# Convolutions on zero-padded or stacked rows in place of 32-row matmuls, and image 1 prepared later

## The reference, cut to what matters

```python
x = x + L0(gn(x), ...)      # gn: mean and variance over the 48x48 of each channel
x = x + dct2(gn(x))         # 48x48 cosine transforms along both axes

# in L0, per image
embed_w  = prelu(Wa @ x + ba)              # 32 -> 32 channels, full size; 6x6 patches, stride 2
match_in = prelu(W1 @ x + b1)              # 32 -> 16 channels, full size; 3x3 patches (queries)
ref      = prelu(W2 @ mean2x2(x) + b2)     # 32 -> 16 channels, 24x24; 3x3 patches (576 keys)
norm     = maximum(sqrt(sum(w * w)), 1e-4) # one per key
yi       = softmax(10 * (w / norm) @ queries, over the 576 keys)   # 576 x 2304
yt       = transposed convolution of yi with the patches of embed_w
yd       = (conv3x3(yt, Wd, stride 2) + bd) / 6
```

## Time and profile before

| | |
|---|---|
| median of 3 runs | 312.26 us (311.34 to 315.21) |
| the profiled execution | 313.37 us, of which its span is 311.6 us |
| mean granted TensorE clock | 0.863 of full |
| busy share of the span | PE 82%, PEld 76%, DVE 51%, ACT 42%, POOL 31% |
| instructions | 4697, 1698 of them matmuls |

### The profile page before, as it was taken

How to read it: one execution, slowest core, us unless ns; L and a number is a source line. 1 busy time by engine, 2 the same in 40 slices (tenths; PEclk the granted TensorE clock), 3 DMA queues, 4 the chain that set the end, 5 groups by cost and what they waited for, 6 DMA issues and landing times.

```text
span 311.6 us, 4697 instructions
## 1 busy us (share of the span) xinstructions
PE 255.3 (82%) x1698; PEld 237.3 (76%) x1698; DVE 160.0 (51%) x343; ACT 130.9 (42%) x257; POOL 96.8 (31%) x98
## 2 busy tenths in 40 slices
PE   0458749966599999959989999999989899997085
PEld 0336748955588889949989899999978799996073
DVE  7544163247544363662266446467787664434722
ACT  2053035376346662442256846365646422121020
POOL 6220150077265343144041344339619200000000
PEclk9999999576555895985799999999999999999555
DMA  3430444000003004440000000000300000000321
GB/s 91 108 52 1 70 72 68 1 1 0 3 0 52 2 0 69 68 70 6 2 0 3 0 2 0 2 1 0 78 1 2 0 2 2 0 2 1 63 50 38
DMA packets 11494, 7.67 MB, mean 25 GB/s; under 512 B 8496, under 2 KB 10608, under 8 KB 11344
## 3 DMA queue, kind: packets, MB, share of 16 engines
q1 hardware_dynamic: 11168, 6.94, 12.3%
q10 hardware_dynamic: 304, 0.45, 0.4%
HBM read 2.14 MB, written 1.18 MB: 11 GB/s over the span
## 4 chain that ended last, share of the span: by engine, by line
PE 62%; DVE 21%; issue 8%; ACT 7%; POOL 1%; DVEq 0%; ACTq 0%; POOLq 0%
PE zt L730 21%; PE ps L710 8%; PE yt L745 8%; PE pm L662 6%; PE pm L622 4%; DVE negm L1174 3%; PE pm L684 3%; PE pm L777 3%; DVE yl L1189 3%; PE pd L757 2%; DVE bnst L993 2%; ACT nt L899 2%; DVE v L1212 2%; PE zt L710 2%; PE pm L693 2%
## 5 line engine op out<-in xcount | busy, mean ns | idle before, releaser
L730 PE MATMUL zt<-ident,nt 128*125 128x128 f32 (+1 forms) x720 | 94.8, 284 | 0.0
L730 PEld LDWEIGHTS zt<-ident,nt 128*125 128x125 f32 (+1 forms) x720 | 90.8, 186 | 1.1 <-issue 0.2
L526 POOL TENSOR_TENSOR nt<-nt 128x599 f32<-128x599 f32 (+1 forms) x42 | 56.2, 1338 | 46.9 <-ACT nt L907 39.7
L1189 DVE TENSOR_TENSOR yl<-zt,yh 125x384 fp32r<-125x384 f32 (+1 forms) x60 | 33.4, 556 | 46.6 <-ACT yh L915 15.3
L915 ACT ACTIVATE yh<-zt 125x384 fp32r<-125x384 f32 (+1 forms) x60 | 29.2, 487 | 46.9 <-PE zt L730 46.8
L899 ACT ACTIVATE nt<-ps,negm 128x576 f32<-128x576 f32 x32 | 23.8, 745 | 47.5 <-DVE negm L1174 47.5
L907 ACT ACTIVATE nt<-nt,rps 128x599 f32<-128x599 f32 x36 | 28.7, 798 | 11.8 <-DVE rps L1181 11.5
L516 POOL TENSOR_TENSOR ml<-vim,mh 128x384 fp32r<-128x384 f32 x12 | 12.3, 1029 | 65.3 <-ACT mh L871 65.2
L745 PE MATMUL yt<-yh,kh 125*128 125x384 f32 (+1 forms) x60 | 24.7, 411 | 7.1 <-DVE yl L1189 7.0
L1212 DVE SCALAR_TENSOR_TENSOR v<-pd,v 32x384 f32<-32x384 f32 (+3 forms) x48 | 26.2, 547 | 4.1 <-PE pd L757 2.7
L1174 DVE TENSOR_REDUCE negm<-ps 128x1 f32<-128x576 f32 x32 | 24.1, 753 | 7.6 <-PE ps L710 7.5
(11 more groups left out here) (160 smaller groups left out, 433.1 us busy)
## 6 DMA issues: line engine op xcount, KB each, us to landing
vim<-mimg SPq DMA_DIRECT2D x24, 72.0 KB, 2.5
v<-mimg SPq DMA_DIRECT2D x36, 24.0 KB, 1.9
v<-x SPq DMA_DIRECT2D x2, 288.0 KB, 4.0
vim<-mimg SPq DMA_DIRECT2D x12, 48.0 KB, 2.2
x_copy<-v SPq DMA_DIRECT2D x2, 288.0 KB, 3.1
xr<-x_copy SPq DMA_DIRECT2D x4, 144.0 KB, 2.9
out<-res SPq DMA_DIRECT2D x8, 72.0 KB, 2.2
x<-x SPq DMA_DIRECT2D x6, 72.0 KB, 2.0
```

The source lines that it names most:

```text
L526: pool.tensor_tensor(nt[:, dst, (to + 1) * KP + 1:(to + 1) * KP + 1 + n], nt[:, one, (row1 + 1) * KP + 1:(row1 + 1) * KP + 1 + n], nt[:, o ...
L730: last = nc.tensor.matmul(turned(zt[:, m % 2, :], n, dh, col, JW), keys_at(tile, r + dr, n, shift), ident[:, :], start=at == 0, stop=at == ...
L1189: nc.vector.tensor_tensor(yl[0:n, blk, :].rearrange("p (h j) -> p h j", j=W), turned(zt[:, m % 2, :], n), F(yh[0:n, blk, :]).rearrange("p ...
```

## The change

- **Convolutions of image 0.** conv1 and conv2 contract all 128 rows of x4 (or of its pooled form x2) with weights that are zero outside one quarter (wb1, wb2). They are plain f32 matmuls, one a group or half group, and x is not split for them.
- **Convolutions on stacked parts.** x of an image is loaded three times into 96 rows (x3f). x3 holds its high part in rows 0 to 31 and 64 to 95, and its low part in rows 32 to 63; the weights hold high, high and low. One fp32r matmul of 96 rows gives the sum of the three products. embed of both images and conv1 of image 1 use it; embed has 4 matmuls of 288 columns a group. New jobs are xh (ACT, two halves), xl (DVE, two halves) and wst (DVE).
- **Row sums.** POOL adds the squares of three rows in two additions (sv), and norm has 6 matmuls.
- **Biases.** Three jobs in place of one, placed where each is needed. That of embed is one f32 matmul.
- **Banks.** Ahead of the loop the groups rotate over four banks (pm, yt, pd).
- **Keys.** Scaling, high and low parts go in two halves.
- **Zeroing.** The edges of the tiles (nt), mr and wr are zeroed by ACT; before, POOL and DVE did this.
- **Queues.** x4 is one buffer, so that x of image 1 is loaded after conv1 of image 0. The three copies of image 0 take that place in SP's order, those of image 1 stand behind the patches of image 0. The ninth taps of block 0 are started by ACT. POOL's preparation of the output weights comes after the query splits.
- **Later.** The jobs of image 1 move by up to 5 thirds of a step.

```diff
-    ("xs", (0,)), ("mean", (0,)), ("weights", (0,)), ("bias", (0, 1)), ("conv2", (0, 1)), ("low", (0,)),
+    ("xs", (0,)), ("mean", (0,)), ("weights", (0,)), ("bias_2", (0,)), ("conv2", (0, 1)), ("bias_1", (0,)),
     ("conv1", (0, 1)), ("squares", (0,)), ("conv1", (2, 3, 4, 5, 6, 7)), ("norm", (0,)),
-    ("inorm", (0, 1)), ("keys", (0,)), ("split", (0, 1)), ("bias", (2,))]
+    ("inorm", (0, 1)), ("ninth", (0,)), ("xh", (0, 1)), ("keys", (0, 1)), ("split", (0, 1))]
 
 
 SPREAD = [
-    ("emb", 0, 2, 4, 2), ("ek", 0, 2, 9, 2), ("xs", 1, 1, 13, 1), ("mean", 1, 1, 15, 1), ("weights", 1, 1, 19, 1),
-    ("bias", 1, 3, 22, 1), ("residual", 0, 1, 28, 1), ("conv2", 1, 2, 26, 1), ("low", 1, 1, 27, 1),
-    ("conv1", 1, 8, 29, 1), ("squares", 1, 1, 31, 1), ("norm", 1, 1, 37, 1), ("inorm", 1, 2, 40, 1),
-    ("keys", 1, 1, 42, 1), ("emb", 1, 2, 46, 2), ("ek", 1, 2, 51, 2), ("residual", 1, 1, 60, 1),
+    ("wst", 0, 1, 1, 1), ("xl", 0, 2, 1, 1), ("bias_a", 0, 1, 3, 1), ("emb", 0, 2, 6, 3), ("ek", 0, 2, 12, 2),
+    ("xs", 1, 1, 16, 1), ("mean", 1, 1, 19, 1), ("xh", 1, 2, 20, 1), ("xl", 1, 2, 22, 1), ("weights", 1, 1, 22, 1),
+    ("bias_2", 1, 1, 24, 1), ("wst", 1, 1, 25, 1), ("bias_1", 1, 1, 26, 1), ("conv2", 1, 2, 26, 1), ("bias_a", 1, 1, 28, 1),
+    ("residual", 0, 1, 28, 1), ("conv1", 1, 8, 30, 1), ("squares", 1, 1, 30, 1), ("norm", 1, 1, 35, 1),
+    ("inorm", 1, 2, 39, 1), ("keys", 1, 2, 42, 1), ("emb", 1, 2, 47, 2), ("ek", 1, 2, 52, 2), ("residual", 1, 1, 60, 1),
     ("stats", 0, 6, 91, 1), ("deviation", 0, 1, 98, 1), ("x1n", 0, 3, 102, 2), ("zn", 0, 3, 108, 1),
...
-            x4 = [tmp(f"x4_{b}", [128, QUARTER]) for b in range(B)]
-            x4h = tmp("x4h", [128, QUARTER], F32R)
-            x4l = tmp("x4l", [128, QUARTER], F32R)
+            x4 = [tmp("x4", [128, QUARTER])] * B
+            x3f = tmp("x3f", [96, Q])
+            x3 = tmp("x3", [96, Q], F32R)
...
             return ap.bitcast(F32)
 
+        def bank(n):
+
+            if n < nbefore:
+                return (pm[:, 0, :], pm[:, 1, :], yt[:, :], pd[:, :])[n % 4]
...
+                if b:
+                    sp.wait_ge(s_mf, misc_no["conv1", b - 1, ROWS - 1] + 1)
...
+            def load_copies(b):
+
+                if b:
+                    sp.wait_ge(s_xl[b - 1], 2)
+                for k in range(3):
+                    sp.dma_start(x3f[C * k:C * (k + 1), :],
+                                 x[b].rearrange("c h w -> c (h w)")).then_inc(s_x3[b], 16)
...
             load_x(0, range(2))
             output_weights()
-            load_x(1, range(4))
+            load_copies(0)
             for b in range(B):
                 sp.dma_start(x1(b), x[b].rearrange("c h w -> c (h w)")).then_inc(s_xin[b], 16)
             sp.dma_start(cosm[:, :], dct).then_inc(s_cos, 16)
             ref_patches(0)
+            load_x(1, range(4))
             match_patches(0)
+            load_copies(1)
...
-                pool.memset(nt[:, :, 0:KP], 0.0).then_inc(s_tiles, 1)
-                pool.memset(nt[:, :, PT - KP - 2:], 0.0).then_inc(s_tiles, 1)
-                pool.memset(strided(nt[:, 0, :], KP, (PT, NTILES), (KP, HL)), 0.0).then_inc(s_tiles, 1)
...
                 pool.wait_ge(s_sqp[b], 1)
+                pool.wait_ge(s_sq[b], 2)
+                link(pool.tensor_tensor(sv[:, :], sq[:, 1:1 + L], sq[:, 1 + WL:1 + WL + L], ALU.add))
+                pool.tensor_tensor(sv[:, :], sv[:, :], sq[:, 1 + 2 * WL:1 + 2 * WL + L], ALU.add).then_inc(s_sv[b], 1)
+                pool.wait_ge(s_sv[b], 1)
...
+            def bias_2(b, _):
+
+                pe.wait_ge(s_wb2[b], 1)
+                o = misc("bias_2", b, 0)
+                nc.tensor.matmul(o[0:96, 0:1], wb2[:, 0, :], gm[b][:, 2:3], start=True, stop=True).then_inc(s_mf, 1)
...
                 for k in range(2):
-                    q = 2 * i + k
-                    rows = slice(C * q, C * (q + 1))
-                    if k:
-                        other_rows(last)
-                    last = conv(o[0:96, REFQ * k:REFQ * (k + 1)], q, S_W2, 96, x2h[rows, :], x2l[rows, :])
+                    last = nc.tensor.matmul(o[0:96, REFQ * k:REFQ * (k + 1)], wb2[:, 2 * i + k, :], x2[:, :],
+                                            start=True, stop=True)
                 last.then_inc(s_mf, 1)
 
             def conv1(b, i):
-                if i == 0:
-                    pe.wait_ge(s_wst[b], 1)
-                    pe.wait_ge(s_x4l[b], 1)
+
                 o = misc("conv1", b, i)
-                q, cols = i // 2, slice(HALF * (i % 2), HALF * (i % 2 + 1))
-                rows = slice(C * q, C * (q + 1))
-                conv(o[0:96, 0:HALF], q, S_W1, 96, x4h[rows, cols], x4l[rows, cols]).then_inc(s_mf, 1)
+                if b == 0:
+                    pe.wait_ge(s_wb1, 1)
+                    pe.wait_ge(s_x4[b], 16 * 4)
+                    last = nc.tensor.matmul(o[0:96, 0:HALF], wb1[:, i // 2, :],
+                                            x4[b][:, HALF * (i % 2):HALF * (i % 2 + 1)], start=True, stop=True)
+                else:
+                    pe.wait_ge(s_wst[b], 2)
+                    pe.wait_ge(s_xl[b], i // 4 + 1)
+                    last = nc.tensor.matmul(o[0:96, 0:HALF], wst1[:, :], x3[:, HALF * i:HALF * (i + 1)], start=True,
+                                            stop=True)
+                last.then_inc(s_mf, 1)
 
             def embed(b, i):
 
-                pe.wait_ge(s_wst[b], 2)
+                pe.wait_ge(s_wst[b], 1)
+                pe.wait_ge(s_xl[b], i + 1)
                 o = misc("emb", b, i)
-                for k in range(2):
-                    q = 2 * i + k
-                    rows = slice(C * q, C * (q + 1))
-                    if k:
-                        other_rows(last)
-                    dst = o[:, REFQ * k:REFQ * (k + 1)]
-                    parts = [v[rows, :].rearrange("p (i u j v) -> p i u j v", u=2, j=WL, v=2) for v in (x4h, x4l)]
-                    for n in range(4):
-                        at = S_WA + C * (3 - n)
-                        for m, (w, v) in enumerate(((wsh, 0), (wsh, 1), (wsl, 0))):
-                            last = nc.tensor.matmul(dst, w[rows, at:at + 128], parts[v][:, :, n // 2, :, n % 2],
-                                                    start=n + m == 0, stop=n == 3 and m == 2)
+                v = x3[:, HALFQ * i:HALFQ * (i + 1)].rearrange("p (i u j v) -> p i u j v", u=2, j=WL, v=2)
+                for n in range(4):
+                    at = C * (3 - n)
+                    last = nc.tensor.matmul(o[:, 0:HALF], wsta[:, at:at + 128], v[:, :, n // 2, :, n % 2],
+                                            start=n == 0, stop=n == 3)
...
                 for n in range(6):
-                    for r in range(3):
-                        at = WL * r + 96 * n + 1
-                        last = nc.tensor.matmul(o[0:96, n:n + 1], sq[:, at:at + 96], ones[0:96, 0:1], start=r == 0,
-                                                stop=r == 2)
...
+                zero(nt[:, :, 0:KP], s_tiles)
+                zero(nt[:, :, PT - KP - 2:], s_tiles)
+                zero(strided(nt[:, 0, :], KP, (PT, NTILES), (KP, HL)), s_tiles)
+                zero(mr[:, :, :], s_zero)
+                for b in range(B):
+                    zero(wr[b][:, :], s_zero)
...
+            def x3_high(b, i):
...
                 if b:
                     act.wait_ge(s_mf, misc_no["emb", b - 1, 1] + 1)
-                nc.scalar.activation(x4h[:, :], x4[b][:, :], ACT.Copy).then_inc(s_x4h[b], 1)
-                act.wait_ge(s_x2[b], 1)
-                nc.scalar.activation(x2h[:, :], x2[:, :], ACT.Copy, scale=0.25).then_inc(s_x2h[b], 1)
+                cols = slice(HALFQ * i, HALFQ * (i + 1))
+                nc.scalar.activation(x3[:, cols], x3f[:, cols], ACT.Copy).then_inc(s_xh[b], 1)
...
+            def ninth_taps(b, _):
+
+                act.wait_ge(s_const, 6)
+                act.wait_ge(s_mimg[b], 1)
+                at = 1 + 2 * CHUNK + SHIFTS[2][0]
+                for n in range(3):
+                    nc.scalar.dma_start(v2[CR * n:CR * (n + 1), 0:CHUNK],
+                                        mimg[64:64 + CR, at:at + CHUNK]).then_inc(s_mim[0], 16)
...
-            def keys_high(b, _):
-                wait_emptied(act, "inorm", b, 1)
+            def keys_high(b, i):
+
                 if b == 0:
-                    act.wait_ge(s_zero, 4)
-                nc.scalar.activation(wh[b][:, :], wim[:, :], ACT.Copy).then_inc(s_whi[b], 1)
-                nc.scalar.activation(wr[b][0:48, :], wim8[0:48, :], ACT.Copy).then_inc(s_whi[b], 1)
+                    act.wait_ge(s_zero, 3)
+                cols = slice(HALF * i, HALF * (i + 1))
+                act.wait_ge(s_wsc[b], i + 1)
+                nc.scalar.activation(wh[b][:, cols], wim[:, cols], ACT.Copy).then_inc(s_whi[b], 1)
+                wait_emptied(act, "inorm", b, i)
+                nc.scalar.activation(wr[b][0:48, cols], wim8[0:48, cols], ACT.Copy).then_inc(s_whi[b], 1)
```

(41 more changed lines are left out.)

199 lines of the change are left out of this document (92 added, 107 removed).

## The result

The changed kernel takes 275.98 us (median of 4 runs, 275.36 to 277.19), against 313.05 us (311.34 to 315.21) for the kernel before beside it: a ratio of 0.8817, with a 95% interval of 0.8750 to 0.8885. The profiled execution took 275.58 us, its span 273.8, and the mean granted clock is 0.875. The same kernel, run again with the last experiments, gave 276.96 us and 0.8904 (0.8861 to 0.8946).

What follows compares the result with a forecast made beforehand. Bounds: a serial chain of waits ahead of the loop, then image 1's work and PE's half clock in the loop. Savings of 14.0 + 1.2 + 23.2 = 38.4 from 313.4 give 275.0, median 274 us; range 265 to 284, widened to 262 to 292.

Steps and rivals of the forecast that it cites:

- The start: Everything ahead of the loop: first scores at 31.0 us in place of 45.0, 14.0 us earlier, 10 to 16 by bounds.
- The copy's price: DVE's table copy at the start: 0.4 us instead of 3.16 once zeroing of nt leaves POOL for ACT.
- its low end: Wide f32 matmul groups in image 0's conv1: 0.57 us each at half clock, against a high end of 1.13.
- Tiles 0 to 9: First loop stretch, with image 0's embedding: 35.5 us in place of 36.75, bounds 32 to 41.
- Tiles 9 to 18: Loop stretch with image 1's work: 50 us in place of 73.2, 23.2 less, bounds 46 to 60.
- add 1 for waits on DVE and ACT: Term for tiles 9 to 18: 1 us of waits, raising the estimate from 49 to 50 us.
- DVE and ACT take over: Rival: the loop gives back what PE saved, only the part ahead of it is won; 298 us, chance 0.13.
- the rival of a low clock: Rival: in tiles 9 to 18 the 23 us at half clock stay as they are; 284 us, chance 0.17.
- my rule: PE's clock falls with 32-row matmuls; of 23 other half-clock us in tiles 9 to 18, 8.6 us would be saved.
- a sign of being wrong: Half clock on PE with no 32-row matmul in sight would count against the forecast.
- The rest: The run after tile 18: untouched, no change, 154.3 us before and predicted.
- Slower or nothing: Rivals: bare loop loses its clock, 336 or 399 us, chance 0.03; or start gain lost, 306 to 318, chance 0.06.

Runs made afterwards that it cites:

- the fitted kernel: The changed kernel with image 0's low part of x, weight stack and residual ahead of the loop, high part before ACT's DMAs: 273.01 us, 0.8795.
- with 144 columns: The changed kernel with 24 matmuls of 144 columns per embedding group instead of 4 of 288: 286.97 us contracting 96 rows, 291.34 us contracting 32.
- with 288 columns: The changed kernel with 24 matmuls of 288 columns per embedding group instead of 4: 295.55 us contracting 96 rows, 297.96 us contracting 32.
- sums on PE: The changed kernel with row sums as 36 one-column PE instructions again, without POOL's additions, for both images: 281.55 us, 0.9051.

## Why the prediction was right, and where it was not

**The total.** 274 was forecast and 275.98 measured; the sum of the steps was -38.4, and the span lost 37.8. Two terms were off by 3.4 and 4.65 us in opposite directions and nearly cancelled, and a start 1.0 us late met a rest 1.6 us short. That the total is within 2 us is luck to this extent.

**The start (14.0 forecast, 13.0 measured).** Right step by step: each was met to 0.4 us up to the weights, and to 1.2 from the match image on. The term that came out too small is the bias of conv1, by its sloped form: 1.13 us beside POOL's squares, where the same operation took 0.15 without them. ACT waits for it ahead of its first group, and the rest of the start stays about 1 us late. The copy's price (0.4) is 0.34 by measurement; undoing it costs 2.6 us, undoing the four banks 2.4. The f32 matmul was taken at its low end (0.57 a group at half clock) and is near the high one (0.96). That is the four passes that the Trainium skill, "FP8 and Floating Point Precision", section TensorE Precision Notes, has for true FP32: the trace agrees at half clock, for 4 times 288 columns at 1.2 GHz are 0.96 us; at full clock they would be 0.48, and the groups took 0.61. As forecast it moved the sum little, since ACT and DVE were behind it anyway, and the clock rose on the way. ACT's three DMAs and high part ended at 26.9 where 25 was forecast, and the first half of the keys was scaled by then.

**Tiles 0 to 9 (35.5 forecast, 32.1 measured).** The named terms were right: the four halves of the low part took 6.0 us (6.4 forecast), the weights wb 1.49, the embedding 1.27 and 1.20 in place of 9.22. The failed step is the sum, which took all of image 1's preparation to stay in the stretch where it had been. Its statistics, weights and biases were moved by 2 to 4 thirds, and the sum left that out: the stack of the weights and two biases of image 1 stand on DVE behind tile 9 now (67.2 to 70.3 us), where all weights and two biases stood ahead of it before. Moving the jobs back by 3 put 6.3 us into this stretch, more than the 3.4 us that the forecast missed, for it took along some that had not stood there before, the first group of conv2 among them. Work moved past a milestone leaves one sum and enters the next.

**Tiles 9 to 18 (50 forecast, 54.65 measured).** The PE side of the sum held in total: 15.6 of work and 8.6 of clock were to go, 24.2 together, and PE's busy time fell by 24.8, from 68.4 to 43.6 (to 46.2 in the repeated run). Its parts held less well. The work put in takes 8.8 us where 6.0 was forecast: the eight matmuls of the embedding 2.47 where 1.3 was taken, the eight f32 instructions of conv2 1.93 for 0.96, and conv1 2.44 for 1.3. The clock and the work that stayed gave more in return. The failed step is "add 1 for waits on DVE and ACT". PE idled 4.6 us in this stretch before, 3.5 of it by the wait on yl, and 11.4 and 10.8 in the two profiles after, by the three waits shown above. DVE and ACT were busy for 34.3 and 33.9 of 55 us, so there was room by shares. But each group of conv1 is a chain from PE to ACT to DVE, and with two banks in the loop PE can have to wait for the end of it from the third group on; two groups did, for 4.0 us. The wait for the weights of conv1's bias (3.4) stands in this stretch by the same omission as above: with the jobs of image 1 three thirds earlier it falls ahead of tile 9, PE idles 7.8 us here in place of 10.8, and the stretch is 4.5 us shorter. That is nearly the whole miss, so jobs that crossed the boundary and waits of side work are not two causes that add up, and their shares are not separated. This was the rival "DVE and ACT take over" at a fifth of its size (4.65 of 24.8 us); it was priced as all or nothing.

**The clock.** The forecast asked for 0.9 or more in this stretch; 0.91 and 0.85 were seen in two executions, 0.86 in the fitted kernel. Time at half clock was taken as 36.1 us there before; the windows of the earlier trace rows leave out 3.4 us at half clock from 150.9, so that it was 39.5. The forecast left 5.8, the rival of a low clock 23, and 9.9 and 17.1 were measured. So this step lies between the two, nearer to the forecast in one profile and to the rival in the other. That rows of a matmul count, beside how long PE is busy, was shown twice: with 144 columns the clock stayed full through the second group of image 0 with 96 rows and fell with 32, and with 288 columns PE was busy for 94% of 17 us at 0.80 with 96 rows, and for all of them at 0.50 with 32. The Trainium skill, "TensorE: Matmul & The Clock Gate", section What's actually happening, ties the clock to how busy TensorE has been; the trace disagrees, if busy means occupied. But my rule, that 32-row matmuls make it fall, was too narrow. It also fell behind one-column matmuls (sums on PE), in the second embedding with 96 rows, and stood at 0.65 from 31 to 66 us in the changed kernel, whose only 32-row matmul there is a bias of one column (0.38 us). That last is what I had named as a sign of being wrong. It cost little because PE was busy for only 23 of these 35 us. What starts each of these falls is not settled: rows were separated from count and from occupancy, idle time ahead of the fall was not. The times of the falls differ between two executions of one program, so a window of a single profile is weaker evidence than the mean clocks of four runs.

**The rest.** 1.6 us less than forecast in the first profile and 2.2 less in the repeated one. No run looked into it.

**Slower or nothing.** Neither happened; the bare loop kept a clock of 1.00 for 129 us.

## What to carry to other kernels

Count matmuls before rows: a product of split parts on stacked rows turns three instructions into one (here, with groups twice as wide, six into one) and saved more than the clock did, 9 to 12 us of the embedding against 4.5. When an engine loses a third of its work, follow the chain through the others for one unit of side work, and price its waits from that and not from shares of busy time. Look at what each small operation on a chain will run beside: one of 96 values cost 1 us there. When jobs move in a written order, set up each stretch's sum by the jobs that will be in it, not by those that were.
